# Raising the expert stage's semaphores from a drain behind TensorE's last product, in an attention and mixture-of-experts layer

## The chip, the cores and the metric

The kernel runs on one core of one Trainium2 chip. The time is that of one execution on the device in microseconds; the median of several runs is compared.

## The reference

The layer is an adaptive layer norm around linear attention, and a second one around eight experts of which each token takes two. Cut to what matters for the change (8 batches of 1024 tokens, width 128, hidden width 256):

```python
h = layernorm(x) * (1 + ca) + sa
x = x + ga * attention(h)                    # linear attention with rope and a 5-tap convolution
h = layernorm(x) * (1 + cb) + sb
probs = softmax((h @ Wg + bg) / 5.0)
vals, idx = top_k(probs, 2)                  # gates: the two kept, divided by their sum
h = gelu(einsum('bsd,edh->besh', h, W1) + b1)
out = einsum('besh,ehd->besd', h, W2) + b2
x = x + gb * einsum('bse,besd->bsd', gates, out)
```

The kernel computes the experts only for the tokens that chose them.

## The kernel before, in words

Every engine has an instruction stream of its own, and each stream is written by a call of `schedule(stage)`: a table, `AT` with `BEGIN` and `BEGIN_EXPERTS`, gives each stage of each batch a tick, and all engines emit their part of the stages in the order of the ticks (`BY_TICK`). So on TensorE the attention stages of a later batch stand between the expert stages of an earlier one, in a fixed order, and the engines are held together by semaphores alone.

The attention part of a batch (`xT`, `qkv`, `vT`, `kv`, `qT`, `den`, `dn`, `gate`, `out`) and the routing (`x1T`, `logit`, `prefix`, `gT`) share three PSUM banks, which `bank_free` guards (its wait is L329). GpSimd then scatters the normalised tokens into `x_sort` in DRAM, sorted by expert and padded to 23 tiles of 128 tokens (L637); SyncE brings them back in groups of four tiles as `xg` (L298) and each tile's expert weights as `wbuf` (L289, a ring of 8).

The expert part on TensorE has three kinds of stage:

- `xsT`, 6 a batch: up to 4 transposes of a group into `ps_x` (L439). `s_xsT` releases ScalarE's `xs_t` (L564) and SyncE's next `xg`.
- `l1`, 12 a batch, each a couple of tiles with 2 products a tile into `ps_hid` (L451). `s_l1` releases ScalarE's GELU (L574), which writes `hid`.
- `l2`, 12 a batch, each a couple of tiles with 2 products a tile that add into `ps_o` (L462). `s_l2` releases ScalarE's copy `o_s` (L582), the ring of `wbuf` on SyncE, and `hid`.

The data is float32, and the trace has two records for each product of L451 and L462, one for each transpose of L439. Each record has a weight load (PEld) and a matmul (PE). The three stages begin with waits (L435, L437; L443, L445, L448; L456, L458); where one instruction has several semaphores to wait for, the program has a wait instruction of the sequencer ahead of it, which the trace lists under the line of the wait. The results go through `o_s` to `o_sort` in DRAM (L590), GpSimd gathers the two rows of each token (`og`, L647), and VectorE adds them up with the gates (L833, L836) on top of the bias product `ps_z` (L470).

Of the kernel before, what the change touches and what calls it, by code (L numbers as in the profile page):

```python
# [89 lines left out]
def adaln_moe_kernel(nc, x, wqkvg, wo, wmod, c_t, lepe, w_route, b_route, w_all, b2, rope, consts, out):  # L90
    with ExitStack() as ctx:
# [232 lines left out]
        def _(pe):  # L324
# [6 lines left out]
            def stage(b, kind, n):  # L331
# [17 lines left out]
                elif kind == "vT":  # L349
                    pe.wait_ge(s_v, J * (b + 1))  # L350
                    for c in range(CH):
                        bank_free(f"vT_{c}", b)
                        for j in range(JC):
                            last = pe.transpose(of(f"vT_{c}", b)[:, j * P:(j + 1) * P], v[:, c * JC + j, 0:D], ident)
                        last.then_inc(s_vT, 1)
                elif kind == "kv":
                    pe.wait_ge(s_qk, J // 2 * (b + 1))
                    bank_free("kv", b)
                    for j in range(J):
                        last = pe.matmul(of("kv", b)[:, 0:D + 1], qk[:, j, D:2 * D], v[:, j, :], start=(j == 0),  # L360
                                         stop=(j == J - 1))
                    last.then_inc(s_kv, 1)
                elif kind == "qT":
                    pe.wait_ge(s_qk, J // 2 * (b + 1))
                    for c in range(CH):
                        bank_free(f"qT_{c}", b)
                        for j in range(JC):
                            last = pe.transpose(of(f"qT_{c}", b)[:, j * P:(j + 1) * P], qk[:, c * JC + j, 0:D], ident)
                        last.then_inc(s_qT, 1)
                elif kind == "den":  # L370
                    pe.wait_ge(s_kvs, b + 1)
                    pe.wait_ge(s_qt, CH * (b + 1))
                    bank_free("den", b)
                    for j in range(J):
                        last = pe.matmul(of("den", b)[:, j * HEADS:(j + 1) * HEADS], q_t[:, j * P:(j + 1) * P],  # L375
                                         ksum_s[:, :], start=True, stop=True)
                    last.then_inc(s_den, 1)
                elif kind == "dn":
                    t = slice(n * CT, (n + 1) * CT)
                    bank_free(f"num_{n}", b)  # L380
                    pe.matmul(of(f"num_{n}", b)[:, :], kv_s[:, :], q_t[:, t], start=True, stop=True).then_inc(s_nm, 1)  # L381
                    pe.wait_ge(s_rx, CH * b + n + 1)
                    bank_free(f"rden_{n}", b)
                    for j in range(JC):
                        k = (n * JC + j) * HEADS
                        last = pe.transpose(of(f"rden_{n}", b)[:, j * P:(j + 1) * P],
                                            rden_x[:, k:k + HEADS, :].rearrange("p h d -> p (h d)"), ident)
                    last.then_inc(s_rT, 1)
                elif kind == "gate":
                    bank_free(f"gate_{n}", b)  # L390
                    pe.matmul(of(f"gate_{n}", b)[:, :], wqkvg_f[:, 3 * D:], h1[i][:, n * CT:(n + 1) * CT], start=True,  # L391
                              stop=True).then_inc(s_gate, 1)
                elif kind == "out":
                    if b == 0 and n == 0:
                        pe.wait_ge(s_wog, 1)
                    pe.wait_ge(s_ot, CH * b + n + 1)
                    bank_free(f"out_{n}", b)
                    for j in range(JC):
                        t = n * JC + j
                        last = pe.matmul(of(f"out_{n}", b)[:, j * P:(j + 1) * P], heads[:, t * P:(t + 1) * P], wo_g[:, b, :],  # L400
                                         start=True, stop=True)
                    last.then_inc(s_out, 1)
                elif kind == "x1T":
                    pe.wait_ge(s_xn2, CH * b + n + 1)
                    bank_free(f"x1T_{n}", b)
                    for j in range(JC):
                        last = pe.transpose(of(f"x1T_{n}", b)[:, j * P:(j + 1) * P], xn2[i][:, n * JC + j, :], ident)
                    last.then_inc(s_x1T, 1)
                elif kind == "logit":
                    if b == 0:  # L410
                        pe.wait_ge(s_w["small"], 6 * 16)
                    pe.wait_ge(s_h2, CH * (b + 1))
                    bank_free("logit", b)
                    for j in range(J):
                        last = pe.matmul(of("logit", b)[:, j * E:(j + 1) * E], h2_t[:, j * P:(j + 1) * P], wr_f[:, :],  # L415
                                         start=True, stop=True)
                    last.then_inc(s_lg, 1)
                elif kind == "prefix":
                    if b == 0:
                        pe.wait_ge(s_tri, 1)  # L420
                    pe.wait_ge(s_route, ROUTE * b + 13)
                    bank_free("prefix", b)
                    pos = of("prefix", b)[:, 0:(J + 1) * E]
                    pe.matmul(pos, before[:, :], chosen[:, :], start=True, stop=False)
                    for k in range(1, J + 1):
                        last = pe.matmul(pos[:, k * E:], every[:, :], chosen[:, 0:(J + 1 - k) * E], start=False,
                                         stop=(k == J))
                    last.then_inc(s_pos, 1)
                elif kind == "gT":
                    pe.wait_ge(s_route, ROUTE * b + 24)  # L430
                    bank_free("gT", b)
                    pe.transpose(of("gT", b)[0:J * E, 0:P], gates[:, :, :].rearrange("p j e -> p (j e)"), ident).then_inc(s_gT, 1)
                elif kind == "xsT":
                    k = group(b, n)
                    pe.wait_ge(s_xg[k % XG_RING], ring_count(k, XG_RING))  # L435
                    if k >= 1:
                        pe.wait_ge(s_xs, k)  # L437
                    for t in range(min(GROUP, TILES - n * GROUP)):
                        last = pe.transpose(ps_x[:, t * P:(t + 1) * P], xg[k % XG_RING][:, t, :], ident)  # L439
                    last.then_inc(s_xsT, 1)  # L440
                elif kind == "l1":
                    k, g = couple(b, n), group(b, 2 * n // GROUP)
                    pe.wait_ge(s_xs, g + 1)  # L443
                    if k >= 2:
                        pe.wait_ge(s_gelu, k - 1)  # L445
                    for m in couple_tiles(n):
                        w = nth(b, m)
                        pe.wait_ge(s_wb[w % W_RING], ring_count(w, W_RING))  # L448
                        t = slice(m % GROUP * P, (m % GROUP + 1) * P)
                        for h in range(HH):  # L450
                            last = pe.matmul(ps_hid[k % 2][:, m % 2, h, :], wbuf[w % W_RING][:, h * P:(h + 1) * P],  # L451
                                             xs_t[g % XS_RING][:, t], start=True, stop=True)
                    last.then_inc(s_l1, 1)
                elif kind == "l2":
                    k, g = couple(b, n), group(b, 2 * n // GROUP)
                    pe.wait_ge(s_gelu, k + 1)  # L456
                    if g >= 1:
                        pe.wait_ge(s_oe, g)  # L458
                    for m in couple_tiles(n):
                        w = nth(b, m)  # L460
                        for h in range(HH):
                            last = pe.matmul(ps_o[:, m % GROUP, :], hid[k % HID_RING][:, m % 2, h, :],  # L462
                                             wbuf[w % W_RING][:, HID + h * D:HID + (h + 1) * D], start=(h == 0),
                                             stop=(h == HH - 1))
                    last.then_inc(s_l2, 1)
                elif kind == "b2":
                    pe.wait_ge(s_gt, b + 1)
                    if 2 * b + n >= 1:
                        pe.wait_ge(s_comb, J * b + n * JC)
                    pe.matmul(ps_z[:, :], gates_t[b % LAG][:, :], b2_f[:, n * CT:(n + 1) * CT], start=True, stop=True)\  # L470
                        .then_inc(s_b2, 1)
# [459 lines left out]
```

## Time and profile before

| | us |
|---|---|
| median of 3 runs | 488.49 (486.08 to 492.94) |
| the profiled execution | 489.41 |
| its span, first to last instruction | 487.5 |
| PE busy, of the span | 408.9 (84%) |
| PEld, DVE, ACT, POOL busy | 341.1, 329.3, 297.4, 299.1 |

PE is TensorE's matmul, PEld its weight load, DVE is VectorE, ACT ScalarE, POOL GpSimd, SP SyncE. PE's instructions overlap in the array, and their ends are modelled, so its busy time is the time with at least one in flight. A `q` behind an engine's name marks an instruction of its sequencer alone (waits, drains, DMA issues); those do not count as busy. PEclk is the granted clock as a share of 2.4 GHz. A row of the timeline gives start, duration, engine, line, operation and the tiles out<-in, then the idle time in front of it and what ended it; "issue" is idle time for which the profile shows no releaser.

### The profile page before, as it was taken

What the parts mean: (1) busy time and instruction counts of PE and PEld (TensorE: products, weight loads), DVE (VectorE), ACT (ScalarE), POOL (GpSimd) and SP (SyncE); (2) the same over time, 40 slices, a digit from 0 to 9 for tenths busy, and PEclk for the clock granted to TensorE, in tenths of its full rate; (3) what the DMA queues carried; (4) which work ended last, traced back from release to release, by engine and by line L of the source; (5) the groups of instructions that cost most, each with busy time, mean ns of one, the idle gap of its engine ahead of it and who ended that gap; (6) DMA issues with size and microseconds to landing.
All of it is one profiled execution on the core that took longest, in us unless ns stands there. A gap on an engine that the chain in (4) does not pass through costs nothing.

```text
span 487.5 us, 9883 instructions
## 1 busy us (share of the span) xinstructions
PE 408.9 (84%) x2808; PEld 341.1 (70%) x2808; DVE 329.3 (68%) x1070; ACT 297.4 (61%) x805; POOL 299.1 (61%) x293
## 2 busy tenths in 40 slices
PE   2578787599999999999999999999988969688410
PEld 2355374288899879887988798879877857587200
DVE  3297987897787588988988898778864710333342
ACT  1454553488679687868786878587566644465200
POOL 0320127717623787878787877777787777737671
PEclk9998876999999999999999998999999997899755
DMA  7920501489988798888998897779889998999521
GB/s 238 298 79 2 167 2 43 129 238 282 280 248 250 226 269 253 260 235 266 273 262 236 266 300 225 233 218 309 244 254 283 283 319 245 266 289 312 153 74 39
DMA packets 113845, 107.81 MB, mean 221 GB/s; under 512 B 10040, under 2 KB 85440, under 8 KB 113536
## 3 DMA queue, kind: packets, MB, share of 16 engines
q1 hardware_dynamic: 80848, 77.76, 54.8%
q0 software_dynamic: 8192, 16.79, 11.3%
q10 hardware_dynamic: 24752, 12.64, 8.6%
q8 instruction: 23, 0.38, 0.3%
q14 instruction: 30, 0.25, 0.2%
HBM read 76.47 MB, written 30.68 MB: 220 GB/s over the span
## 4 chain that ended last, share of the span: by engine, by line
PE 58%; POOL 11%; DMA 10%; DVE 7%; ACT 6%; issue 6%; SPq 1%; POOLq 0%; ACTq 0%; DVEq 0%
PE ps_hid L451 13%; PE ps_o L462 12%; PE bank L347 6%; POOL x_sort L637 5%; POOL og L647 4%; PE ps_x L439 3%; DMA o_sort<-o_s 3%; ACT xn L489 3%; PE bank L360 3%; PE ps_z L470 3%; PE bank L415 2%; DMA og<-o_sort,slots 2%; PE bank L381 2%; PE bank L391 2%; PE bank L375 2%
## 5 line engine op out<-in xcount | busy, mean ns | idle before, releaser
L637 POOL DMA_INDIRECT x_sort<-xn,slots x128 | 138.1, 1079 | 65.0 <-issue 36.6
L647 POOL DMA_INDIRECT og<-o_sort,slots x128 | 126.6, 989 | 48.1 <-issue 44.4
L574 ACT ACTIVATE hid<-ps_hid,wbuf 128x128 f32<-128x128 f32 x368 | 104.5, 374 | 33.0 <-PE ps_hid L451 27.2
L451 PE MATMUL ps_hid<-xs_t,wbuf 128*128 128x128 f32 x736 | 101.6, 282 | 7.4 <-DMA wbuf<-in_w_all 4.3
L462 PE MATMUL ps_o<-wbuf,hid 128*128 128x128 f32 x736 | 99.3, 283 | 4.9 <-ACT hid L574 3.9
L451 PEld LDWEIGHTS ps_hid<-xs_t,wbuf 128*128 128x128 f32 x736 | 92.6, 195 | 13.4 <-issue 5.6
L462 PEld LDWEIGHTS ps_o<-wbuf,hid 128*128 128x128 f32 x736 | 91.2, 196 | 13.4 <-issue 6.6
L833 DVE SCALAR_TENSOR_TENSOR u<-og,gate,ps_z 128x128 f32<-128x128 f32 x64 | 22.0, 343 | 72.8 <-DMA og<-o_sort,slots 47.4
L613 POOL TENSOR_TENSOR rstd<-var_eps,minus_half 128x8 f32<-128x8 f32 x16 | 27.2, 1700 | 61.8 <-DVE var_eps L668 61.6
L347 PE MATMUL bank<-wqkvg_f,h 128*128 128x384 f32 x128 | 51.4, 527 | 7.5 <-ACT v L514 6.5
L564 ACT ACTIVATE xs_t<-ps_x,mod 128x512 f32<-128x512 f32 (+1 forms) x48 | 37.3, 777 | 18.1 <-PE ps_x L439 17.9
L760 DVE SCALAR_TENSOR_TENSOR conv<-v_t,lepe_f,conv 128x1024 f32<-128x1024 f32 x32 | 40.7, 1272 | 0.2
L777 DVE TENSOR_TENSOR qk_cos<-bank,rope_f 128x256 f32<-128x256 f32 x64 | 26.8, 419 | 19.6 <-PE bank L347 19.5
L347 PEld LDWEIGHTS bank<-wqkvg_f,h 128*128 128x128 f32 x128 | 23.2, 204 | 23.6 <-ACT v L514 12.4
L582 ACT ACTIVATE o_s<-ps_o 128x512 f32<-128x512 f32 (+1 forms) x48 | 28.2, 588 | 13.3 <-PE ps_o L462 10.1
L514 ACT ACTIVATE v<-bank 128x128 f32<-128x128 f32 x64 | 16.4, 276 | 30.3 <-DVE qk_sin L779 30.3
L489 ACT ACTIVATE xn<-xs,shift,rstd 128x128 f32<-128x128 f32 x64 | 26.1, 494 | 13.8 <-POOL shift L615 13.8
L470 PE MATMUL ps_z<-b_f,gates_t 64*128 64x512 f32 x32 | 21.1, 744 | 13.3 <-DVE u L836 13.3
L439 PE MATMUL ps_x<-consts_f,xg 128*128 128x128 f32 x184 | 28.3, 275 | 4.1 <-DMA xg<-x_sort 3.8
L489 ACT ACTIVATE xn<-x,shift,rstd 128x128 f32<-128x128 f32 x64 | 26.3, 493 | 2.9 <-POOL shift L615 2.9
L439 PEld LDWEIGHTS ps_x<-consts_f,xg 128*128 128x128 f32 x184 | 21.5, 142 | 7.8 <-DMA xg<-x_sort 4.0
L779 DVE TENSOR_TENSOR qk_sin<-bank,rope_f 128x256 f32<-128x256 f32 x64 | 26.5, 414 | 0.0
(122 smaller groups left out, 629.1 us busy)
## 6 DMA issues: line engine op xcount, KB each, us to landing
wbuf<-in_w_all SPq DMA_DIRECT2D x184, 257.0 KB, 3.6
xg<-x_sort SPq DMA_DIRECT2D x40, 256.0 KB
o_sort<-o_s ACTq DMA_DIRECT2D x40, 256.0 KB
x_sort<-zero SPq DMA_DIRECT2D x20, 256.0 KB, 4.4
xs<-in_x SPq DMA_DIRECT2D x8, 512.0 KB, 5.6
out<-y SPq DMA_DIRECT2D x16, 256.0 KB
x_sort<-xn,slots POOLq DMA_INDIRECT x128
og<-o_sort,slots POOLq DMA_INDIRECT x128, 4.3
```

What stands on the lines that cost most here:

```text
L347: pe.matmul(of(f"qkv_{j}", b)[:, 0:3 * D], h1[i][:, t], wqkvg_f[:, 0:3 * D], start=True, stop=True)\
L439: last = pe.transpose(ps_x[:, t * P:(t + 1) * P], xg[k % XG_RING][:, t, :], ident)
L451: last = pe.matmul(ps_hid[k % 2][:, m % 2, h, :], wbuf[w % W_RING][:, h * P:(h + 1) * P], xs_t[g % XS_RING][:, t], start=True, stop=True)
L462: last = pe.matmul(ps_o[:, m % GROUP, :], hid[k % HID_RING][:, m % 2, h, :], wbuf[w % W_RING][:, HID + h * D:HID + (h + 1) * D], start=(h ...
L470: pe.matmul(ps_z[:, :], gates_t[b % LAG][:, :], b2_f[:, n * CT:(n + 1) * CT], start=True, stop=True)\
L489: last = act.activation(dst[:, j, :], src[:, j, :], ACT.Identity, bias=shift[n][:, j:j + 1], scale=rstd[n][:, j:j + 1])
L564: act.activation(xs_t[k % XS_RING][:, 0:many * P], ps_x[:, 0:many * P], ACT.Identity, bias=mod[:, 3, b:b + 1], scale=mod[:, 4, b:b + 1]).t ...
L574: last = act.activation(hid[k % HID_RING][:, m % 2, h, :], ps_hid[k % 2][:, m % 2, h, :], ACT.Gelu, bias=w[:, 2 * HID + h:2 * HID + h + 1])
L582: act.activation(o_s[k % O_RING][:, 0:many, :], ps_o[:, 0:many, :], ACT.Copy).then_inc(s_oe, 1)
L637: pool.indirect_dma_start(x_sort[b % SORTS], bass.IndirectOffsetOnAxis(ap=at, axis=0), xn2[i][:, n, :], None).then_inc(s_scat[b % SORTS], 16)
L647: pool.indirect_dma_start(og[:, k, n, :], None, o_sort[i], bass.IndirectOffsetOnAxis(ap=at, axis=0)).then_inc(s_gat[n], 16)
L760: dve.scalar_tensor_tensor(conv[:, :], v_t[:, k:k + S], lepe_f[:, k:k + 1], conv[:, :], ALU.mult, ALU.add)\
```

## The change

In each of the three expert stages the semaphore's increment is taken off the last transpose or product and put on a drain instruction of TensorE that follows it. The conditions that others wait for, the order of the products and all other stages stay as they are.

```diff
@@ -437,7 +437,7 @@
                     for t in range(min(GROUP, TILES - n * GROUP)):
                         last = pe.transpose(ps_x[:, t * P:(t + 1) * P], xg[k % XG_RING][:, t, :], ident)
-                    last.then_inc(s_xsT, 1)
+                    pe.drain().then_inc(s_xsT, 1)
                 elif kind == "l1":
@@ -450,7 +450,7 @@
                             last = pe.matmul(ps_hid[k % 2][:, m % 2, h, :], wbuf[w % W_RING][:, h * P:(h + 1) * P],
                                              xs_t[g % XS_RING][:, t], start=True, stop=True)
-                    last.then_inc(s_l1, 1)
+                    pe.drain().then_inc(s_l1, 1)
                 elif kind == "l2":
@@ -462,7 +462,7 @@
                                              wbuf[w % W_RING][:, HID + h * D:HID + (h + 1) * D], start=(h == 0),
                                              stop=(h == HH - 1))
-                    last.then_inc(s_l2, 1)
+                    pe.drain().then_inc(s_l2, 1)
```

## Rows read from the trace of the kernel before

**Rows 1.** Busy time of each engine by stretch, granted clock, DMA share, GB/s.

```profile
core 0: us, PE busy (x) PEld busy (x) DVE busy (x) ACT busy (x) POOL busy (x), PEclk, DMA share, GB/s
100.00:356.00 256.00, 254.98 (x1910) 223.05 (x1910) 209.83 (x673) 196.60 (x538) 182.27 (x174) 0.99 0.88 257
356.00:412.00 56.00, 47.04 (x341) 41.14 (x339) 22.52 (x83) 32.38 (x95) 43.42 (x44) 0.94 0.92 275
412.00:456.00 44.00, 34.66 (x245) 29.89 (x245) 11.83 (x29) 23.44 (x68) 27.52 (x29) 0.96 0.95 286
```

**Rows 2.** Waits of PE from 100 to 356 us: total us, times, longest.

```profile
PE bank L432 <- DVE ksum_s L790: 0.6, 1, 0.6
PE ps_x L439 <- ACT xs_t L564: 0.3, 1, 0.3
```

**Rows 3.** Two lines' own pages: records, ns min/median/max.

```profile
L451 PE MATMUL ps_hid<-xs_t,wbuf x736: 272/275/582, 104.4 to 451.8; 128*128 128x128 f32 x184
...
L439 PE MATMUL ps_x<-consts_f,xg x184: 272/273/332, 102.1 to 447.2; 128*128 128x128 f32 x184
```

**Rows 4.** Order of time on PE, in the bound stretch.

```profile
237.38 1.50 PE L451 MATMUL ps_hid<-xs_t,wbuf 128*128 128x128 f32 x12
```

**Rows 5.** PE and PEld busy by stretch: of L439, then L451, then L462.

```profile
100.00:356.00 256.00, 20.00 (x131) 15.31 (x131) 0.99 0.88 257
356.00:412.00 56.00, 4.67 (x30) 3.63 (x30) 0.94 0.92 275
...
100.00:356.00 256.00, 68.07 (x508) 62.85 (x508) 0.99 0.88 257
356.00:412.00 56.00, 18.07 (x124) 16.10 (x124) 0.94 0.92 275
...
100.00:356.00 256.00, 64.25 (x492) 59.93 (x492) 0.99 0.88 257
356.00:412.00 56.00, 19.45 (x132) 17.23 (x132) 0.94 0.92 275
```

**Rows 6.** Order of time, 446.9 to 450 us.

```profile
447.29 1.06 PE L451 MATMUL ps_hid<-xs_t,wbuf 128*128 128x128 f32 x8
...
448.07 0.97 PEld L462 LDWEIGHTS ps_o<-wbuf,hid 128*128 128x128 f32 x8
...
448.38 1.14 ACT L574 ACTIVATE hid<-ps_hid,wbuf 128x128 f32<-128x128 f32 x4 [0.22 <-PE ps_hid L451]
...
449.57 0.97 PEld L462 LDWEIGHTS ps_o<-wbuf,hid 128*128 128x128 f32 x8 [0.53 <-ACT hid L574]
```

**Rows 7.** The last product of PE in time, and its sequencer's drain (L91).

```profile
470.61 2.04 PE L470 MATMUL ps_z<-b_f,gates_t 64*128 64x512 f32 x2 [10.07 <-DVE u L836]
...
L91 PEldq DRAIN  x1: 2070/2070/2070, 470.6 to 470.6; - x1
```

**Rows 8.** The drain ahead of the program, nothing in flight.

```profile
L924 PEldq DRAIN  x1: 8/8/8, 0.3 to 0.3; - x1
```

**Rows 9.** Wait instructions of TensorE's sequencer: l1's and the banks'.

```profile
L448 PEldq EVENT_SEMAPHORE  x96: 51/51/51, 104.3 to 451.0; - x96
...
L329 PEldq EVENT_SEMAPHORE  x133: 51/51/1335, 23.3 to 407.7; - x133
```

**Rows 10.** The chain that ended last, start and duration, 412 to 458 us.

```profile
420.07 2.08 PE ps_hid L451 x8
422.15 1.75 PE ps_o L462 x12
...
449.57 1.16 PE ps_o L462 x8
450.73 0.91 PE ps_hid L451 x8
```

**Rows 11.** Busy time of each engine in two halves of 356 to 412.

```profile
356.00:384.00 28.00, 23.42 (x183) 20.53 (x182) 15.53 (x65) 17.54 (x50) 21.95 (x23) 1.00 0.93 278
384.00:412.00 28.00, 23.62 (x160) 20.61 (x158) 7.00 (x19) 14.84 (x45) 21.48 (x22) 0.88 0.91 271
```

## The prediction

> **What bounds the kernel now.** I read the stretches first, then the waits of TensorE, then the chain. The table of stretches [rows 1] splits the span: from 100 to 356 us TensorE's products are busy 254.98 of 256 us at a granted clock of 0.99; from 356 to 412 us they are busy 47.04 of 56, and from 412 to 456 us 34.66 of 44. Behind it TensorE has little more than the last bias product, at 470.61 us [rows 7]. TensorE's waits say the same: in the first stretch they are two, of 0.9 us together [rows 2]. So there is a bound stretch, in which every nanosecond that TensorE loses is added to the end, and a tail of 100 us in which it has 9 and 9.3 us of idle time and much else (GpSimd's scatters and gathers, DMA landings) sits on the chain. One caution: an end is modelled as 0.275 us behind a start [rows 3], while 12 products of L451 that follow each other last 1.50 us from the first start to the last end, so they start every (1.50 - 0.275)/11 = 0.111 us [rows 4]. "Busy" therefore means in flight, two and a half deep; a gap of up to 0.16 us between starts would not show as idle. At the joint of two stages in rows 6 (L451 to L462, 448.07 us) there is none, so I take the engine as filled to its cadence there.
>
> **What the change does, and how often.** Each expert batch has 6 groups (xsT), 12 couples (l1) and 12 couples (l2), over 8 batches 48 + 96 + 96 = 240 drains. Nothing else moves: the order of the products is the same. By records, a drain of L439 stands behind 184/48 = 3.83 of them, one of L451 or L462 behind 736/96 = 7.67 [rows 3] (L462 has 736 like L451). The bound stretch holds 131, 508 and 492 records of L439, L451 and L462 [rows 5], so 34 + 66 + 64 = 164 drains; 356 to 412 us holds 30, 124 and 132, so 41; the rest, 35, stand in 412 to 456 us.
>
> **What one drain costs.** Today the weight load for the next stage starts as the stage's last product starts: L462's loads begin at 448.07 us, and L451's last product begins at 447.29 + 1.06 - 0.275 = 448.075 us [rows 6]. A drain has to see TensorE empty. The only row of a drain behind running products is that at the program's end: it starts at 470.6 us and takes 2070 ns, to 472.67 or 472.70 us, while the product in front of it ends at 470.61 + 2.04 = 472.65 us [rows 7]. It waits for the product and goes about 0.04 us beyond. With nothing in flight it takes 8 ns [rows 8]. Then the sequencer takes the next instruction. All three stages begin with a wait instruction on the sequencer, 51 ns each [rows 9] (l1's line, x96; xsT's and l2's read alike with 47 and 94); today it runs ahead under the products, behind a drain it cannot. Last comes the start of the weight load: ScalarE's last GELU ends at 448.38 + 1.14 = 449.52 us and the load that waited for it starts at 449.57 us [rows 6], 0.05 us, semaphore included. The sum:
> - last product in flight: 0.275 us (cold clock aside)
> - the drain's own end: 0.04
> - the wait instruction: 0.05
> - restart of the weight load: 0.05
> - together 0.415 us, where today it is 0; I take 0.41.
>
> Bounds: nothing below zero, since no instruction goes and none comes earlier. At least 0.275 us, if the drain ends with the product and issue is immediate. At most 0.56: a second wait instruction (stages on a bank have one of L329, x133 [rows 9]) and the push of the semaphore ahead of the next instruction, 0.05 each, and 0.05 for what I don't see. I take 0.41 because each of its four parts has a row. That is the price where TensorE would have gone on at once; where it waits for something later anyway, that wait hides it. The drain's semaphore rises some 0.04 us later than the product's own; in the bound stretch ScalarE's and VectorE's idle time covers that.
>
> The Trainium skill ("PSUM — Partial Sum Buffer", section "Engine vs sequencer instructions") says that a drain waits for the engine to go fully idle. The trace agrees in the one drain that it shows, those 2070 ns. Another page of the Trainium skill, "TensorE: Matmul & The Clock Gate" (section "Single matmul latency") gives an isolated 128-column product as (398 + 128)/2.4, an estimate of 0.219 us; with that in place of 0.275 a drain would cost 0.36 us and the bound stretch 59 us. The row has the duration, so it is used.
>
> **The sum.** Bound stretch: 164 x 0.41 = 67 us, less the 1 us that is idle there. No cover: TensorE is the cover that everything else uses. 356 to 412 us: 41 x 0.41 = 17 us against 9 us of idle TensorE and a chain that goes through GpSimd's queue of scatters and gathers (POOL busy 43.42 of 56) [rows 1]; 17 - 9 = 8 is what is left if all idle time absorbs, near 0 if the chain stays off TensorE. I take 5. 412 to 456 us: in the chain I count nine places at which a drained stage is followed by another piece of TensorE [rows 10] (the first of them is L451 to L462 at 422.15 us, the last L462 to L451 at 450.73 us); 9 x 0.41 = 3.7 us, and some five handoffs at 0.04 us: 4 us. Behind 456 us: nothing. Sum: 66 + 5 + 4 = 75 us, on the profiled execution's 489.4 us (span 487.5 and 1.9 around it): 564.4. The median of the runs is 488.5, 0.9 lower; I keep **565 us** between rounding and the profiled base, some 16% over before.
>
> Its own range: with 0.275 us 164 x 0.275 = 45 - 1 + 3 = 47, so 536 us; with 0.56 us 92 - 1 + 7 + 5 = 103, so 592 us.
>
> **The rivals.**
> 1. *The clock falls (worse).* The drains put a gap of 0.4 us into TensorE's work every 1 us or so. Between 384 and 412 us, with products busy 23.62 of 28 us, the granted clock is 0.88; from 356 to 384 us, with 23.42 of 28, it is 1.00 [rows 11]. So the clock can fall at a busy share of the kind that the change makes, and need not. Of the two levels 1.2 and 2.4 GHz, 0.88 means 24% of the time at the lower. If the bound stretch went from 0.99 to 0.88, its 255 us of work would take 255 x 0.99/0.88 = 287, 32 us more: about 597 us. The Trainium skill's page "TensorE: Matmul & The Clock Gate" (section "A second HAM failure mode: psum-queue depth-cycling") describes a kernel whose short idle times between groups of matmuls made the clock oscillate; by that rule the 597 us of this case would be the result. The trace agrees with it in one of the two stretches (0.88) and not in the other (1.00).
> 2. *The drain does not hold the weight loads behind it (not slower).* It would only order the semaphore: the place is the hand-over from l1 to GELU and from l2 to the copy, the price the 8 ns of a drain with nothing in front [rows 8], 240 x 0.008 = 2 us, 491 us. It decides below 9.8/164 = 0.06 us a drain. For it: the sequencer runs ahead of TensorE today, and a queue of loads might be refilled in the shadow. Against it: a sequencer that sits in a drain until the engine is empty has nothing in the queue when it leaves.
> 3. *Other limits cover it (slower, but little).* The DMA engines' share is 0.88 in the bound stretch [rows 1], and if the transfers set the pace, TensorE's bubbles would fall into waits that come anyway. Against it: no wait on a DMA stands among TensorE's in that stretch [rows 2]. If half were covered: 34 + 5 = 39 us, 528 us.
> 4. *The restart is long.* If the sequencer has to fetch again and needs 0.8 us a drain: 164 x 0.8 = 131, with the tail 145, 634 us. Nothing in the rows speaks for it.
>
> **How the numbers follow.** The forecast 0.73; the clock 0.12; no hold 0.06; half covered 0.04; long restart 0.05. Range 537 to 602 us: it holds nearly all of the forecast and most of the clock's case; the other three lie outside, 0.15, with a little from the edges. 2% is about what a measurement of this kernel can tell from no change, 9.8 us. Slower by over 2%: all but the second rival, 0.93 (rounded down, since unknown covers may add up); within 2%: 0.06; faster: 0.01, as no term has that sign.
>
> **What would show it.** In the profile after: drains of 300 ns or more behind L439, L451 and L462; at each, the next weight load 0.41 us behind the start of the last product where it was 0; waits of PE that carry no releaser but "issue", about 240 of them; ScalarE and VectorE busy as before but idle longer; the stretch in which TensorE is bound about 320 us long in place of 256; the tail from the last expert product to the end unchanged (about 33 us). The forecast falls if drains end before the products do (rival 2), if the granted clock of the bound stretch is under 0.95 (rival 1), or if the gap at a drain is under 0.3 or over 0.6 us.

## The result and the profile after

| | before | with the drains |
|---|---|---|
| median of 5 runs, us | 488.56 (486.08 to 492.94) | 585.01 (577.4 to 604.5) |
| ratio | | 1.187, 95% interval 1.18 to 1.194 |
| the profiled execution, us (span) | 489.41 (487.5) | 604.5 (602.6) |
| mean granted clock of that execution | 0.934 | 0.884 |

The forecast was 565 us in a range from 537 to 602. The time lies inside, on the high side: 96 us were added by the medians (91 by the ratio, 0.187 x 488.56), where 76 had been forecast. One thing is needed to read the traces: the profiled execution is the longest of the five, at the lowest clock; the one of 577.4 us had 0.936, those of 582.16 and 585.01 us had 0.926 and 0.922. Part of its 115 us is therefore clock, and I estimate below how much. The execution of 577.4 us, at nearly the clock of the profiled execution of before (0.934), is 89 us over the median of before.

TensorE issues the same products in the same order, so the two traces can be cut at the same product. The first cut is the one at 100.3 us before, the second the one at 356.0 us, where TensorE ceased to be the bound. Busy time of each engine, granted clock, DMA share and GB/s, before:

```profile
core 0: us, PE busy (x) PEld busy (x) DVE busy (x) ACT busy (x) POOL busy (x), PEclk, DMA share, GB/s
0.00:100.30 100.30, 68.37 (x314) 46.22 (x314) 73.39 (x263) 45.26 (x109) 30.20 (x31) 0.90 0.40 121
...
100.30:356.00 255.70, 254.73 (x1907) 222.86 (x1908) 209.56 (x670) 196.30 (x537) 182.27 (x174) 0.99 0.88 257
356.00:487.50 131.50, 85.78 (x590) 72.03 (x588) 46.34 (x141) 55.82 (x161) 86.58 (x89) 0.85 0.77 228
```

And after, the same three pieces of work:

```profile
0.00:105.60 105.60, 73.01 (x314) 49.32 (x314) 73.53 (x263) 45.37 (x109) 30.90 (x31) 0.84 0.38 117
...
105.60:446.60 341.00, 305.95 (x1908) 243.40 (x1909) 210.83 (x670) 203.30 (x539) 187.50 (x178) 0.94 0.67 194
446.60:602.60 156.00, 107.09 (x590) 83.22 (x588) 45.75 (x140) 56.33 (x159) 82.02 (x84) 0.78 0.65 188
```

The work is the same in each (1907 and 1908 matmul records, 590 and 590; VectorE's and ScalarE's busy times hardly move). The bound stretch grew by 341.0 - 255.7 = 85.3 us, the tail by 156.0 - 131.5 = 24.5, and the first piece, in which there are no drains, by 5.3. That last one goes with the clock (0.84 against 0.90). The DMA share fell from 0.88 [rows 1] to 0.67: the same transfers are spread over a longer time.

What a drain does is seen best in a quiet piece of the bound stretch after, in the order of time (start, duration, engine, line, tiles, idle time in front):

```profile
258.56 0.60 PE L439 MATMUL ps_x<-consts_f,xg 128*128 128x128 f32 x4
...
259.36 0.97 PEld L451 LDWEIGHTS ps_hid<-xs_t,wbuf 128*128 128x128 f32 x8 [0.44 <-issue]
259.39 1.13 PE L451 MATMUL ps_hid<-xs_t,wbuf 128*128 128x128 f32 x8 [0.23 <-issue]
...
260.58 1.14 ACT L574 ACTIVATE hid<-ps_hid,wbuf 128x128 f32<-128x128 f32 x4 [0.58 <-PEq L453]
260.72 0.97 PEld L462 LDWEIGHTS ps_o<-wbuf,hid 128*128 128x128 f32 x8 [0.39 <-issue]
```

L439's last transpose starts at 258.56 + 0.60 - 0.273 = 258.887 us and the next weight load at 259.36: 0.473 us. L451's last product starts at 259.39 + 1.13 - 0.275 = 260.245, the next load at 260.72: 0.475 us. Before, this distance was nothing at the joint of rows 6. Of it the product's records show 0.23 us as idle; the rest is the pipe running empty, which the modelled ends count as busy. That is why TensorE's busy share in the stretch is still 306 of 341 us though far more is lost.

Where no wait instruction follows the drain, because the next stage has one semaphore to wait for, the distance is shorter. Here L391 follows L451:

```profile
250.67 1.06 PE L451 MATMUL ps_hid<-xs_t,wbuf 128*128 128x128 f32 x8
...
251.80 0.30 PEld L391 LDWEIGHTS bank<-h,wqkvg_f 128*128 128x128 f32 x2 [0.27 <-issue]
```

250.67 + 1.06 - 0.275 = 251.455 to 251.80: 0.345 us. So the wait instruction, a record of 51 ns, costs 0.473 - 0.345 = 0.13 us behind a drain.

These are not picked cases. I measured the distance at all 165 drains of the bound stretch in this trace. Of the 142 with a wait instruction behind them, the 129 at the full clock have 0.473 us in the median and the 13 at the lower level 0.62; the 23 without one have 0.349. Together they make 78 us.

The drains have records of their own; these are l1's (ns min/median/max):

```profile
L453 PEldq DRAIN  x96: 650/1708/3922, 109.7 to 566.9; - x96
```

Their length does not give their cost: 1.7 us in the median, where the hole is 0.473. The sequencer reaches a drain early and sits in it while the queued products run, so I read the 1.7 us as how far it was ahead. The cost is only what comes behind the last product.

### The profile page after: what moved, and what is told of

Same layout as the page of the kernel before. It is cut to its first block, busy times and chain, and to the rows that moved or that the text cites. A ratio compares the mean times of both kernels' runs of the same rounds, so it can differ in the third digit from the quotient of the medians.

```text
span 602.6 us, 10123 instructions
## 1 busy us (share of the span) xinstructions
PE 486.1 (81%) x2808; PEld 375.9 (62%) x2808; DVE 330.1 (55%) x1070; ACT 305.0 (51%) x805; POOL 300.4 (50%) x293
## 4 chain that ended last, share of the span: by engine, by line
PE 33%; PEld 24%; issue 16%; DVE 8%; PEldq 6%; POOL 5%; ACT 4%; DMA 2%; POOLq 0%; SPq 0%; ACTq 0%; DVEq 0%
PEld ps_o L462 8%; PEld ps_hid L451 8%; PE ps_o L462 6%; PE ps_hid L451 6%; PE bank L347 5%; PEldq L453 2%; POOL x_sort L637 2%; PE bank L381 2%; PE bank L400 2%; PEldq L465 2%; ACT xn L489 2%; PEld ps_x L439 2%; POOL og L647 1%; PEldq L440 1%; PE bank L415 1%
## 5 line engine op out<-in xcount | busy, mean ns | idle before, releaser
L451 PE MATMUL ps_hid<-xs_t,wbuf 128*128 128x128 f32 x736 | 114.9, 304 | 14.3 <-issue 11.6
L462 PE MATMUL ps_o<-wbuf,hid 128*128 128x128 f32 x736 | 113.5, 301 | 15.7 <-issue 14.3
L451 PEld LDWEIGHTS ps_hid<-xs_t,wbuf 128*128 128x128 f32 x736 | 101.2, 211 | 30.0 <-issue 25.1
L462 PEld LDWEIGHTS ps_o<-wbuf,hid 128*128 128x128 f32 x736 | 98.6, 207 | 33.8 <-issue 27.3
L347 PE MATMUL bank<-wqkvg_f,h 128*128 128x384 f32 x128 | 54.7, 552 | 12.4 <-ACT v L514 8.2
L439 PE MATMUL ps_x<-consts_f,xg 128*128 128x128 f32 x184 | 31.2, 293 | 7.3 <-issue 5.8
L800 DVE TENSOR_TENSOR heads<-heads,bank 128x512 f32<-128x512 f32 x16 | 11.0, 688 | 41.5 <-ACT heads L544 35.8
L439 PEld LDWEIGHTS ps_x<-consts_f,xg 128*128 128x128 f32 x184 | 21.7, 149 | 16.0 <-issue 14.2
L489 ACT ACTIVATE xn<-x,shift,rstd 128x128 f32<-128x128 f32 x64 | 26.3, 500 | 3.1 <-POOL shift L615 3.1
```

Source lines behind the costliest of these rows:

```text
L347: pe.matmul(of(f"qkv_{j}", b)[:, 0:3 * D], h1[i][:, t], wqkvg_f[:, 0:3 * D], start=True, stop=True)\
L489: last = act.activation(dst[:, j, :], src[:, j, :], ACT.Identity, bias=shift[n][:, j:j + 1], scale=rstd[n][:, j:j + 1])
```

## The experiments

The kernels ran in four sets. Each set had one chip and its own runs of the kernel before, which took 489.74, 666.3, 493.68 and 657.1 us (medians); the first two sets had the same chip. In the traces of the second and fourth set there are stretches in which TensorE stands still for up to 16 us, and VectorE and ScalarE for most of that time, while GpSimd goes on; the kernel before has no trace there, but its time lets me suppose that it has them as well. This is the longest in one trace of the second set:

```profile
463.80 0.50 PE L452 MATMUL ps_hid<-xs_t,wbuf 128*128 128x128 f32 x3
479.81 1.01 PE L347 MATMUL bank<-wqkvg_f,h 128*128 128x384 f32 x1 [15.52 <-remote]
```

I don't know their cause. From these two sets I take distances inside the trace and give totals only for completeness. The two kernels whose totals matter most (5 and 6 below) ran again in the third.

**1. The parts alone.** In each of three kernels one stage has its drain and the two others raise the semaphore from the product as before:

```diff
-                    last.then_inc(s_l1, 1)
+                    pe.drain().then_inc(s_l1, 1)
```

> Only the 96 drains of l1, the other semaphores stay on the products. Theory (each drain costs an empty-and-restart gap of 0.47 us behind the last product's start, against 0.00 before, and TensorE has nothing to cover it): 96/240 of the 91 us that the change cost, 36 us, so 525 us. Rival (what counts is that the hand-over to GELU comes later, on the chain l1 to GELU to l2): nearly all of the 91 us comes from this part, 560 to 580 us.

> Only the 96 drains of l2. Theory: the same number of gaps as l1, so the same 36 us, 525 us. Rival (late hand-over to GELU): l2 hands over to a copy and to a weight ring that have slack, 489 to 500 us.

> Only the 48 drains of the transposes. Theory: 48/240 of 91 us, 18 us, so 507 us. With the two other parts this adds up to 91 us if the gaps are independent; a rival by which the clock falls only once gaps are dense makes the three parts alone add up to clearly less (under 75 us).

Measured: l1 alone 522.34 us (ratio 1.0635, 1.056 to 1.071), l2 alone 531.08 us (520.42 to 532.93; three of its four runs had a clock of 0.914 to 0.924, the one of 520.42 us had 0.941), the transposes alone 507.04 us (1.0361, 1.028 to 1.044). Over 489.74 that is 33, 41 and 17 us, 91 together. The medians flatter this sum: by l2's one run at a clock like the others', 520.42 us, l2 costs 31 us and the three 81. Either way they stay over the 75 us of the rival that lets the clock fall only when the holes are dense, by the lower reading not by much. The same cut at the same products, l1, l2, transposes:

```profile
105.20:387.20 282.00, 268.31 (x1908) 226.54 (x1909) 210.34 (x670) 200.50 (x539) 186.55 (x176) 0.99 0.82 233
387.20:520.70 133.50, 88.59 (x590) 73.69 (x588) 45.74 (x140) 55.96 (x159) 85.41 (x87) 0.84 0.77 223
...
100.40:392.00 291.60, 276.49 (x1908) 233.10 (x1909) 210.21 (x670) 197.65 (x537) 189.07 (x177) 0.96 0.79 227
392.00:530.90 138.90, 93.69 (x590) 76.31 (x588) 46.28 (x141) 55.85 (x161) 83.65 (x86) 0.82 0.74 213
...
101.30:372.40 271.10, 263.08 (x1908) 225.22 (x1909) 209.97 (x670) 198.34 (x538) 182.28 (x175) 0.99 0.84 242
372.40:503.90 131.50, 85.74 (x590) 70.70 (x588) 46.33 (x141) 56.11 (x161) 84.82 (x88) 0.86 0.77 227
```

The bound stretch grows by 26.3, 35.9 and 15.4 us, 77.6 together, for 66, 64 and 34 drains. Per drain this is 0.40, 0.56 and 0.45 us, and l2's stretch has a clock of 0.96 where the others have 0.99. An estimate from these rows: 0.96 in place of 0.99 is 6% more of 291.6 us at the lower level, 17 us; if the work goes at half its pace there, 9 us are lost, and 27 us are left for l2, 0.42 a drain. So the count sets the cost, and not the stage. The rival that blamed the late hand-over to GELU expected l1 at 560 to 580 and l2 under 500 us; both are out. The tail grows by 2.0, 7.4 and 0.0 us, 9.4 together, against 24.5 with all three: there the parts do not add up (the reason is given with the tail below).

**2. Drains that nobody waits for.** All 240 drains, with the semaphores left on the products:

```diff
-                    last.then_inc(s_l1, 1)
+                    last.then_inc(s_l1, 1)
+                    pe.drain()
```

> All 240 drains, but the semaphore stays on the last product, so nobody else gets a later signal. Theory (the gap on TensorE is the cost): as the changed kernel, 580 us, within 6 us. Rival (the later signal is the cost): close to the kernel before, under 510 us.

Measured: 599.13 us, ratio 1.224 (1.217 to 1.232). No hand-over is later here, and the cost is all there, so the rival is dead. My number was 19 us too low, though. Its cut:

```profile
100.00:438.00 338.00, 303.09 (x1908) 240.60 (x1909) 210.82 (x670) 202.63 (x539) 189.49 (x178) 0.95 0.69 196
438.00:593.10 155.10, 107.94 (x590) 83.55 (x588) 45.60 (x140) 56.22 (x159) 81.47 (x84) 0.77 0.66 189
```

Stretch by stretch that is nearly the changed kernel (341.0 and 156.0), and the holes are nearly as long (in the trace 0.460 us in the median with a wait instruction behind the drain, 0.375 without). Its four runs had clocks of 0.889 to 0.896, which in the changed kernel goes with 592.9 (0.903) to 602.6 us (0.884) of span. So the excess goes with a lower clock. Why all four runs had it is open.

**3. Two drains in a row.**

```diff
+                    pe.drain()
                     pe.drain().then_inc(s_l1, 1)
```

> Two drains in a row at each of the 240 places. Theory (a drain waits for the engine to be empty; a second one finds it empty): 240 times a drain with nothing in flight, 0.01 to 0.06 us each, of which about 0.85 is exposed: 2 to 12 us over the changed kernel, 583 to 593 us. Rival (a drain has a fixed price of its own of tenths of a us): 240 x 0.18 x 0.85 = 37 us more, about 617 us.

Second set: 789.88 against 666.3 us (ratio 1.19, 1.18 to 1.21). The records of the two drains of l2, and a joint of l1 and the transposes:

```profile
L468 PEldq DRAIN  x96: 13/13/13, 111.9 to 751.9; - x96
...
178.74 1.14 PE L452 MATMUL ps_hid<-xs_t,wbuf 128*128 128x128 f32 x8
...
180.15 0.42 PEld L439 LDWEIGHTS ps_x<-consts_f,xg 128*128 128x128 f32 x4 [0.47 <-issue]
```

The second drain takes 13 ns in the record, but the next load comes 180.15 - (178.74 + 1.14 - 0.275) = 0.545 us behind the last product's start, 0.07 later than with one (546 ns in the median of l2's drains, against 473). A drain on an empty engine costs 0.07 us, a little over the 0.06 that I had allowed and far from the rival's 0.18; the other 0.40 us of a hole belong to the emptying, the wait instruction and the restart. The ratio of the totals cannot show 240 x 0.07 = 17 us, since the standing still blurs it.

**4. More wait instructions.** Four waits on semaphores that are long met, at the head of each expert stage; l1 then has three wait instructions where it had one. Once on the changed kernel, once on the kernel before:

```diff
+                    for done in ("mod", "ident", "attn", "small"):
+                        pe.wait_ge(s_w[done], {"mod": 32, "ident": 16, "attn": 16, "small": 96}[done])
```

> The changed kernel with four more, long-met waits at the head of each expert stage, two more wait instructions of 51 ns a stage. Theory (behind a drain the sequencer has no lead, so what it does between drain and load is exposed): about half of the 240 drains are followed by an expert stage; 125 x 2 x 0.06 to 0.12 us = 15 to 30 us over the changed kernel, 595 to 610 us. Rival (the sequencer still hides them): no difference, 580 us.

> The kernel before (no drains) with the four more long-met waits at the head of each expert stage. Theory (without drains TensorE's sequencer is ahead of the products and does its wait instructions under them): within 1% of the kernel before, under 5 us. Rival (a wait instruction costs TensorE its time wherever it stands): 480 x 0.05 = 24 us or more over the kernel before.

On the changed kernel (second set) 803.82 us, ratio 1.211 against 1.19 of two drains in a row in the same set. The joint that corresponds to the one above:

```profile
178.42 1.14 PE L455 MATMUL ps_hid<-xs_t,wbuf 128*128 128x128 f32 x8
...
179.97 0.42 PEld L441 LDWEIGHTS ps_x<-consts_f,xg 128*128 128x128 f32 x4 [0.60 <-issue]
```

179.97 - 179.285 = 0.685 us: two wait instructions more are 0.21 us more, 0.105 each. On the kernel before (fourth set) 659.93 against 657.1 us, 0.4% by the medians (ratio 1.013, 0.990 to 1.036, so the total alone does not exclude 24 us). The joint does: l1 behind L360, with its three wait instructions.

```profile
153.98 1.95 PE L360 MATMUL bank<-v,qk 128*128 128x129 f32 x16
155.77 0.50 PE L455 MATMUL ps_hid<-xs_t,wbuf 128*128 128x128 f32 x3
```

16 records at 0.112 us are 1.79 us, and L455 starts 155.77 - 153.98 = 1.79 us after L360. Nothing is lost between the last product of L360 and L455. So at a joint where the sequencer is ahead the waits are free; behind a drain each costs about 0.1 us.

**5. Waiting for the product instead of draining.** TensorE waits for its own semaphore in front of what comes next:

```diff
                     last.then_inc(s_l1, 1)
+                    pe.wait_ge(s_l1, k + 1)
```

> No drain; TensorE waits for its own product's semaphore ahead of the next stage. Theory (the pipe has to run empty, and the instructions behind start late): a product's semaphore comes some 0.29 us behind its start, the weight load 0.03 to 0.05 later, without the wait instruction's 0.12 behind it where that was passed while waiting: 0.32 to 0.47 us a place against 0.47, so 550 to 585 us. Rival (the drain instruction itself is what costs): under 520 us.

> No drain, TensorE waits for its own product's semaphore. The earlier try's trace has the next weight load 0.331 us behind the last product's start, against 0.473 with a drain (0.349 where no wait instruction follows the drain). Theory: the cost goes by that gap, 91 x 0.331/0.45 = 67 us, so 556 us. Rival (a drain is special beyond the gap): under 540 us.

Second set 737.64 against 666.3 us; third set 553.37 against 493.68 us, ratio 1.117 (1.110 to 1.125). The cut, and a joint, of the third set:

```profile
105.40:415.00 309.60, 299.79 (x1908) 235.20 (x1908) 210.76 (x670) 201.01 (x539) 188.14 (x176) 0.98 0.74 213
415.00:554.00 139.00, 98.88 (x590) 75.03 (x588) 45.96 (x140) 56.39 (x160) 83.63 (x87) 0.85 0.73 213
...
176.33 0.60 PE L439 MATMUL ps_x<-consts_f,xg 128*128 128x128 f32 x4
...
176.99 0.97 PEld L464 LDWEIGHTS ps_o<-wbuf,hid 128*128 128x128 f32 x8 [0.29 <-PE ps_x L439]
```

The load comes 176.99 - 176.657 = 0.333 us behind the last transpose's start. The bound stretch grew by 309.6 - 255.7 = 53.9 us, and 164 x 0.333 = 54.6. I had scaled the total to 556 us on a base of 489; the base was 494 and the kernel 553, so it cost 60 where 67 was expected. The drain is not special: a wait for the product's own semaphore lets the pipe run empty too, and costs the length of its hole. The drain's usual hole is 0.14 us longer, and nearly all of that is the wait instruction, since without one the drain's hole is 0.345 us. That the sequencer passes its wait instruction here while it waits anyway is my reading; no run isolates it.

**6. The same time lost without a hole.** No drain; the last product is repeated, or the last transpose, into the same place, four records or 4 x 0.111 = 0.446 us of TensorE at each of the 240 places:

```diff
+                    for _ in range(2):
+                        last = pe.matmul(ps_hid[k % 2][:, m % 2, h, :], wbuf[w % W_RING][:, h * P:(h + 1) * P],
+                                         xs_t[g % XS_RING][:, t], start=True, stop=True)
                     last.then_inc(s_l1, 1)
```

> No drain; at each of the 240 places TensorE repeats its last product or transpose for four more records (4 x 0.111 = 0.45 us) into the same place, with the same result, so that it loses as much time as with a drain but never runs empty. Theory (lost TensorE time alone): 240 x 0.45 = 107 us, of which as much is exposed as of the drains' 113 us (0.81): 87 us, 576 us, with a granted clock of 0.95 or more. Rival (part of the cost is that the clock falls because TensorE runs empty): clearly less than the changed kernel, 555 to 568 us, by as much as the changed kernel loses at the lower clock.

> Four more records of product in place of a drain, 0.446 us of TensorE's time at each of 240 places, never empty; the earlier try of it had every run, that of the kernel before too, some 180 us longer. Theory (lost TensorE time alone decides): the changed kernel's cost scaled by 0.446/0.473, 86 us, about 575 us, with a granted clock over 0.95. Rival (emptiness lowers the clock and that is a good part of the cost): 555 to 567 us, and the lower clock's share in the changed kernel's trace makes up the difference.

> The changed kernel once more, beside the two below on one chip: 577 to 590 us if the chip runs as in the first comparison. If it comes out at 595 to 600, the difference to the kernel whose semaphores stay on the products (599 us) was the chip's; if at 580 to 585 it is that kernel's own.

Second set 737.76 us. Third set 579.64 us, ratio 1.173 (1.166 to 1.179), beside the changed kernel's 589.83 us, ratio 1.190 (1.182 to 1.198). All four runs with the filler had a clock of 0.943 to 0.945; those of the changed kernel 0.899 to 0.922, and the kernel before on this chip 0.920 to 0.934. Cut of the filler, then of the changed kernel in this set:

```profile
100.60:430.60 330.00, 329.81 (x2564) 298.89 (x2565) 211.25 (x670) 202.42 (x537) 185.27 (x178) 0.98 0.70 201
430.60:577.90 147.30, 113.90 (x894) 103.29 (x892) 45.88 (x140) 56.67 (x161) 81.83 (x85) 0.88 0.69 200
...
100.70:440.10 339.40, 304.54 (x1908) 243.35 (x1909) 211.17 (x670) 202.92 (x539) 188.19 (x178) 0.95 0.69 194
440.10:596.50 156.40, 107.46 (x590) 83.22 (x588) 45.79 (x140) 56.37 (x159) 81.83 (x84) 0.78 0.65 188
```

With the filler the bound stretch grows by 74.3 us; 164 x 0.446 = 73.1. So in that stretch TensorE's lost time goes to the end one for one, and nothing else is needed to explain the filler. With drains it grows by 83.7; 164 x 0.473 = 77.6, and 6 us remain, in a stretch whose clock is 0.95 in place of 0.98. In the tail the filler adds 15.8 us and the drains 24.9, at 0.88 and 0.78. The rival that gave emptiness a large part expected 555 to 567 us for the filler and is out; a small part remains. Of the 10 us between the two kernels, 0.027 x 240 = 6.5 us at most is the longer hole; the rest, 4 us or more, goes with the lower clock.

## Why the prediction came out as it did

**The bound.** Right. The stretch that I took as bound [rows 1] passes on what TensorE loses (73.1 us expected from the filler's records, 74.3 measured), and the DMA engines had the reserve that the half-covered rival denied them.

**The count.** Right: 164 drains were forecast for the bound stretch, and its cut has 165.

**The price of one.** Forecast 0.41 us, measured 0.473. The mis-sized term is the wait instruction: I priced it with its record, 51 ns, and behind a drain it costs 0.105 to 0.13 us. The three other parts together are 0.345 us where I had 0.365. In the bound stretch that is 164 x 0.063 = 10 us too little. I also let a wait instruction follow every drain, and 23 of 165 have none. (The prediction's other sum, 0.36 us with the Trainium skill's figure in place of 0.275 us, is farther off; the page gives that figure for bf16, and the products here are float32.)

**The tail.** I took 5 + 4 = 9 us for the 76 drains there; it is 24.5 and 24.9 in the two profiles. The step that failed is that I priced 412 to 456 us by nine places on the old chain, and took 5 us for 356 to 412 us although my own 17 - 9 = 8 was a floor and not an upper bound. TensorE has to fit its work and its lost time into the stretch, whatever the chain was. From [rows 1], with 0.446 us at each place: 47.04 + 41 x 0.446 is 9.3 us over 56, and 34.66 + 35 x 0.446 is 6.3 us over 44, an estimate of 15.6 us, and the filler shows 15.8 without any hole. (That the two are so close is partly chance: the estimate fills all idle time, the filler leaves some.) The rows up to the start of the last expert product show TensorE filling up, before, with the filler, with the drains:

```profile
356.00:454.20 98.20, 80.39 (x584) 70.67 (x582) 34.01 (x111) 55.33 (x160) 70.00 (x72) 0.95 0.94 282
...
430.60:544.80 114.20, 108.14 (x884) 101.57 (x883) 33.59 (x110) 56.18 (x160) 66.63 (x69) 0.97 0.83 241
...
446.60:569.70 123.10, 102.38 (x583) 82.06 (x582) 33.47 (x110) 55.84 (x158) 66.61 (x68) 0.83 0.76 222
```

Of 17.8 us in which no product is in flight the filler leaves 6.1. Each part alone, 14 to 32 drains or 7 to 15 us of holes, fits into those 17.8 us, and adds 0 to 7 us; all three, 36 us, do not. With holes of 0.473 us the same estimate gives 10.4 + 7.2 = 17.6 us. The other 7 us or so of the profiled executions go with a clock of 0.83 here in place of 0.95.

**The clock rival.** Given 0.12 and 32 us. It was neither wrong nor a case of its own. In the two profiled executions of this kernel, each the longest of its set, the clock of the bound stretch fell to 0.94 and 0.95; I had said that the forecast falls under 0.95, so by my own sign the first execution is partly the rival's. The price is not well known. What is left of the growth when each drain is charged its whole hole is 6 to 8 us. The clock rows give more: 0.94 in place of 0.99 is 10% more of 341 us at the lower level, 34 us, of which half, 17 us, would be lost at half the pace (an estimate). Then a drain costs somewhat less than its hole, (85.3 - 17)/164 = 0.42 us, much as in the parts alone. So the clock has 6 to 17 us of the bound stretch in these executions, and some 7 us of the tail. In the longest execution, stretches of the tail ran at the lower of the two levels while products were busy 15.40 of 17 us and 18.25 of 21:

```profile
476.00:493.00 17.00, 15.40 (x57) 11.79 (x55) 6.31 (x17) 5.59 (x15) 13.20 (x13) 0.50 0.71 198
520.00:541.00 21.00, 18.25 (x66) 13.92 (x66) 3.91 (x10) 6.15 (x16) 0.00 (x0) 0.51 0.57 165
```

The kernel's runs now scatter over 27 us where they lay within 7, and the longer ones are those at the lower clock. The rule of the Trainium skill that I had set beside this rival ("TensorE: Matmul & The Clock Gate", section "A second HAM failure mode: psum-queue depth-cycling", on idle times between groups that make the clock change back and forth) holds in this weak form: by the run's own rows 0.94 and 0.95 against 0.98 with the filler. But the semaphore wait of experiment 5 makes as many holes, of 0.333 us, and has 0.98 as well; and why one kernel's runs differ in clock (0.884 to 0.936) stays open.

**Luck.** The forecast of 76 us is best compared with the execution at the clock of before, which added 89. It was some 10 us too low in the price and 9 in the tail, and made up a part of that by charging each drain its full hole. The median came inside the range because the range, widened for the clock's case, had room for these misses; the forecast itself put the clock at nothing.

**The other rivals.** The drain that does not hold the loads (not slower): out, the holes are there at each drain of the bound stretch. The long restart (0.8 us): out, 0.47. Half covered: out.

**What I said would show it.** Drains over 300 ns: yes, but for another reason, as they include the products in front. The distance of 0.41: 0.47. The bound stretch of about 320 us: 341 and 339. The time behind the last expert product unchanged: from the start of L462's last record (454.2 us before, 569.7 after, by the line's own page) to the end of the span it is 33.3 and 32.9 us.

## What to carry to other kernels

In this kernel a drain on a saturated TensorE costs the time that the pipe takes to run empty plus all that the sequencer has to do before the next weight load, 0.345 us and about 0.1 us for each wait instruction behind it, and in the bound stretch nearly all of that time reaches the end. Leave the increment on the last product; where TensorE itself really has to wait for its product, a wait for the product's own semaphore was cheaper (0.33 us). Price such a change as (places in the bound stretch) x (hole). In a stretch with idle time, add TensorE's busy time and all its holes: what goes over the stretch's length is a floor for the growth, even where each part alone is free. And leave some us for the clock.

## What the runs showed of the hardware that I had not expected

- A wait instruction with a record of 51 ns takes 0.105 to 0.13 us from the engine behind a drain (0.473 against 0.345 us, and 0.685 with two more), and nothing at the joint without one (1.79 us for 16 records). A drain on an empty engine has a record of 13 ns and takes 0.07 us.
- A drain's record (1.7 us in the median for l1) is not its cost (0.473 us): it covers the products queued ahead of it.
- The hole itself depends on the clock: 0.473 us in the median at the full clock, 0.62 at the lower level.
- Holes of less than half a microsecond, 240 of them, went with a mean clock of 0.899 to 0.922; about the same time filled with products, on the same chip, with 0.943 to 0.945; the kernel before had 0.920 to 0.934.
- A drain without a semaphore on it and one with it leave holes of nearly the same length (0.460 and 0.473 us), but the four runs without it all had a clock under 0.90. That stays open.
